# Routed expert rows: stores into four row slots per token, or additions into two tables of sums

## The reference

```
x = layernorm(x + attention(x))          # 16 heads of 16 channels, 4 key/value heads, causal
scores = sigmoid(x @ gate_w.T) + gate_b  # 16 experts
weights, indices = top_k(scores, 4); weights /= weights.sum()
shared = (silu(x @ w1_s) * (x @ w3_s)) @ w2_s
expert_e(x) = silu((x @ w1_e) * (x @ w3_e)) @ w2_e          # hidden width 176
x = layernorm(x + shared + sum over the 4 chosen e of weight_e * expert_e(x))
```

## Time and profile before

| | |
|---|---|
| runs of the kernel | 704.01 us median of 3 (700.44 to 706.06) |
| the profiled execution, its own time | 701.06 us |
| its span, first to last instruction | 699.3 us |
| mean granted PE clock | 0.894 of full speed |
| attention and routing | up to about 461 us of the span |
| expert stage | about 461 to 652 us |
| tail | about 652 to 699 us |

### The profile page before, as it was taken

The page is one execution under the profiler, slowest core; times in us unless marked ns, Lnnn a source line. Parts: engine busy times, 40 slices in busy tenths (PEclk is TensorE's granted clock), DMA queues, the critical chain, the costliest instruction groups (busy, mean ns, idle before and its releaser), DMA issues. The chain is left out here.

```text
span 699.3 us, 11914 instructions
## 1 busy us (share of the span) xinstructions
PE 561.5 (80%) x3708; PEld 363.4 (52%) x3708; DVE 454.6 (65%) x944; ACT 348.6 (50%) x759; POOL 307.3 (44%) x461
## 2 busy tenths in 40 slices
PE   4769987998899989589869877468999999999200
PEld 3434452443333544234323236458999999999100
DVE  4265537886775788578558116448777777776594
ACT  1216643566466557545555852235565666665022
POOL 3103324032743254836053731711677776776242
PEclk9959988899999999779798998869999999999655
DMA  4684614000511318212021232631344444441671
GB/s 117 114 186 68 98 42 63 6 25 1 132 40 40 47 43 156 73 40 94 1 74 58 65 88 62 203 97 47 98 136 126 126 128 120 130 131 36 240 300 60
DMA packets 53611, 64.92 MB, mean 93 GB/s; under 512 B 7995, under 2 KB 47310, under 8 KB 53552
## 3 DMA queue, kind: packets, MB, share of 16 engines
q1 hardware_dynamic: 46032, 46.45, 26.6%
q0 software_dynamic: 7104, 17.60, 7.1%
q10 hardware_dynamic: 416, 0.13, 0.1%
HBM read 32.49 MB, written 25.76 MB: 83 GB/s over the span
## 5 line engine op out<-in xcount | busy, mean ns | idle before, releaser
L1008 ACT ACTIVATE prob<-psT 128x512 f32<-128x512 f32 (+3 forms) x384 | 163.4, 496 | 107.3 <-PE psT L1521 101.8
L1230 DVE TENSOR_REDUCE MX<-psS 128x1 f32<-128x640 f32 (+6 forms) x176 | 175.7, 1027 | 47.5 <-PE psS L1556 45.3
L1552 PE MATMUL psS<-KS,QS 96*128 96x512 bf16 (+3 forms) x384 | 107.9, 362 | 18.9 <-DVE MX L1230 15.7
L1521 PE MATMUL psT<-QS,KS 98*128 98x512 bf16 (+3 forms) x384 | 106.5, 347 | 13.1 <-ACT prob L1008 8.2
L921 POOL TENSOR_SCALAR_AFFINE_SELECT prob<-prob 128x512 f32<-128x512 f32 x64 | 41.1, 643 | 139.9 <-ACT prob L1008 139.0
L973 POOL DMA_INDIRECT y_scratch<-ys,dst x80 | 80.9, 1011 | 37.8 <-POOL dst L966 18.7
L1536 PE MATMUL psO<-prob,V 128*32 128x512 f32 (+3 forms) x768 | 85.8, 521 | 8.9 <-POOL prob L921 7.2
L1726 PE MATMUL psH<-wU,xh 128*128 (+1 forms) x384 | 85.1, 345 | 9.3 <-issue 8.9
L892 POOL DMA_INDIRECT xs_scratch<-x1row,slotu x64 | 65.1, 1018 | 29.4 <-DVE slotu L1322 15.2
L1552 PEld LDWEIGHTS psS<-KS,QS 96*128 96x128 bf16 x384 | 34.1, 105 | 81.6 <-DVE MX L1230 46.8
L1726 PEld LDWEIGHTS psH<-wU,xh 128*128 128x128 f32 x384 | 65.3, 198 | 10.1 <-issue 10.1
(11 more groups left out here) (206 smaller groups left out, 983.3 us busy)
## 6 DMA issues: line engine op xcount, KB each, us to landing
xs<-xs_scratch SPq DMA_DIRECT2D x80, 134.0 KB
y<-y_scratch SPq DMA_DIRECT2D x8, 1024.0 KB, 12.3
QS<-qp SPq DMA_DIRECT2D x48, 128.0 KB, 4.6
wU_raw<-in_L_ffn_w_routed_dram SPq DMA_DIRECT2D x32, 176.0 KB, 3.4
xs_scratch<-padrow SPq DMA_DIRECT2D x1, 2144.0 KB
xs_scratch<-padrow SPq DMA_DIRECT2D x16, 134.0 KB
x1row<-in_L_attn_x_dram SPq DMA_DIRECT2D x4, 512.0 KB, 6.4
out_dram<-x1row SPq DMA_DIRECT2D x8, 256.0 KB, 2.1
```

The costliest lines, as they stand in the source:

```text
L1008: nc.scalar.activation(prob[:, step % NPROB, h, 0:HALF - c0], ps[:, 0:HALF - c0], ACT.Exp).then_inc(s_Tfree, 1)
L1230: nc.vector.tensor_reduce(out=MX[:, heads[0]:heads[-1] + 1, i - TH * q], in_=src, op=ALU.max, axis=AX_X).then_inc(s_Sfree, 1)
L1521: mm(ps[:, 0:HALF - c0], KS[b][:, g, j * P:(j + 1) * P], QS[:, QAT[(k // 2) % NSLOT], g % 2 * G + h, c0:HALF], start=True, stop=True).then ...
L1552: mm(ps[:, e * dist + c:e * dist + c + w], QS[0:ROWS, QAT[(k // 2) % NSLOT], g % 2 * G + h, (i - TH * q) * P:(i - TH * q + 1) * P], KS[b][ ...
```

## The change

`y4_scratch` (8192 rows) goes; two tables `y_sums0` and `y_sums1` of 2048 rows, one row per token, take its place. A tile's row is added in memory to the row of its token: tiles t = 0 go to table 0 and tiles t = 1 to table 1. As two additions to one row may not be under way together, each store of a table first waits until the store before it in the same table has landed. Both tables are set to zero first, by two DMAs of 2,048 KB each on SP's queue; the padding write of 2,144 KB moves together with them from behind qload 1 to behind qload 4. The tail loads two rows per token in 16 loads of 256 KB and does two additions where it did three. ACT and DVE wait, before they fill `ys` of pair n, for the store n - 2 of their own table alone.

```diff
-FAR = B * T * TOPK
+FAR = B * T
-    y4_dram = nc.dram_tensor("y4_scratch", (FAR, C), F32, kind="Internal").ap()
+    ya_dram = [nc.dram_tensor(f"y_sums{t}", (FAR, C), F32, kind="Internal").ap() for t in range(2)]
-        y4 = sb("y4", [P, NT, TOPK, C])
+        y2 = sb("y2", [P, NT, 2, C])
...
-                    if s == 1:
+                    if s == 4:
                         sp.wait_ge(s_const, CONSTS)
                         sp.dma_start(xs_dram[NE * REG:NE * REG + NE * P, :].rearrange("(m p) c -> p m c", p=P),
                                      padrow[:, :].unsqueeze(1).to_broadcast([P, NE, ROW])).then_inc(s_pad, 16)
+                        for t in range(2):
+                            sp.dma_start(ya_dram[t].rearrange("(i p) c -> p i c", p=P),
+                                         padrow[:, 0:C].unsqueeze(1).to_broadcast([P, NT, C])).then_inc(s_zero, 16)
...
             sp.wait_ge(s_up, EARLY + NRP)
-            for i in range(NYS):
-                sp.wait_ge(s_ysc[i], 32 * ((NRP - i + NYS - 1) // NYS))
-            y4_rows = y4_dram.rearrange("(i p k) c -> p i (k c)", p=P, k=TOPK)
+            for t in range(2):
+                sp.wait_ge(s_sum[t], 16 * NRP)
             for n in range(NSHP):
-                sp.dma_start(y4[:, 2 * n:2 * n + 2, :, :].rearrange("p i k c -> p i (k c)"),
-                             y4_rows[:, 2 * n:2 * n + 2, :]).then_inc(s_y4[n], 16)
+                for t in range(2):
+                    sp.dma_start(y2[:, 2 * n:2 * n + 2, t, :],
+                                 ya_dram[t][2 * n * P:2 * (n + 1) * P, :].rearrange("(i p) c -> p i c", p=P)).then_inc(s_y2[n], 16)
...
-            nc.gpsimd.iota(x1row[:, :, DT], pattern=[[P * TOPK, NT], [1, TOPK]], base=-FAR, channel_multiplier=TOPK,
+            nc.gpsimd.iota(x1row[:, :, DT], pattern=[[P, NT], [0, TOPK]], base=-FAR, channel_multiplier=1,
...
                     pool.wait_ge(s, EARLY + n + 1)
+                    if n:
+                        pool.wait_ge(s_sum[t], 16 * n)
+                    else:
+                        pool.wait_ge(s_zero, 32)
                     nc.gpsimd.indirect_dma_start(
-                        y4_dram, bass.IndirectOffsetOnAxis(ap=dst[:, n % NSEL, t:t + 1], axis=0),
-                        ys[:, n % NYS, t, :], None, bounds_check=FAR - 1, oob_is_err=False).then_inc(s_ysc[n % NYS], 16)
+                        ya_dram[t], bass.IndirectOffsetOnAxis(ap=dst[:, n % NSEL, t:t + 1], axis=0),
+                        ys[:, n % NYS, t, :], None, bounds_check=FAR - 1, oob_is_err=False,
+                        compute_op=ALU.add).then_inc(s_sum[t], 16)
...
-                    act.wait_ge(s_ysc[n % NYS], 32 * (n // NYS))
+                    act.wait_ge(s_sum[0], 16 * (n - NYS + 1))
...
-                    dve.wait_ge(s_ysc[n % NYS], 32 * (n // NYS))
+                    dve.wait_ge(s_sum[1], 16 * (n - NYS + 1))
...
-                dve.wait_ge(s_y4[n], 16)
-                link(nc.vector.tensor_tensor(y4[:, i, 0:2, :], y4[:, i, 0:2, :], y4[:, i, 2:4, :], ALU.add))
-                link(nc.vector.tensor_tensor(y4[:, i, 0, :], y4[:, i, 0, :], y4[:, i, 1, :], ALU.add))
-                link(nc.vector.tensor_tensor(x1[:, i, :], x1[:, i, :], y4[:, i, 0, :], ALU.add))
+                dve.wait_ge(s_y2[n], 32)
+                link(nc.vector.tensor_tensor(y2[:, i, 0, :], y2[:, i, 0, :], y2[:, i, 1, :], ALU.add))
+                link(nc.vector.tensor_tensor(x1[:, i, :], x1[:, i, :], y2[:, i, 0, :], ALU.add))
```

More of the change, by code:

```diff
@@ L639, in attention_moe @@
         s_sel = sem("s_sel")
-        s_ysc = [sem(f"s_ysc{i}") for i in range(NYS)]
-        s_y4 = [sem(f"s_y4_{i}") for i in range(NSHP)]
+        s_zero = sem("s_zero")
+        s_sum = [sem(f"s_sum{t}") for t in range(2)]
+        s_y2 = [sem(f"s_y2_{i}") for i in range(NSHP)]
         s_shift = sem("s_shift")
```

## The result

747.22 us, the median of 4 runs (745.35 to 748.89), against 704.37 us before: 1.0677 times before, 95% interval 1.0616 to 1.0737. The kernel got slower by 43 us; I had forecast 707.9 us with a range up to 745. The profiled execution has a span of 745.3 us against 699.3 us.

A forecast was written before the change was run, and what follows sets the result against it. PE was taken to set the 4.0 us expert-stage pair, with POOL having no reserve. Terms -11.1 - 2.75 + 17.7 + 0 = +3.85 us on the 704.01 us median gave 707.9 us, range 698 to 745.

The forecast's parts named there:

- Part 4 (b): Expert stage: POOL's own time per adding store stays unchanged at 0.99 to 1.05 us; upper end +0.5 us each.
- rival (B): Expert stage: POOL's store instruction gets longer; 724 us at 0.25 us per store, 742 at half as much again; chance 0.22.
- 2 us of buffer: Expert stage: two buffers of results absorb about 2 us of added POOL time, taken off the rivals' totals.
- Part 4 (a): Expert stage: an adding store lands 3.4 us after its start, costing nothing up to about 3.9 us; 0 us added.
- Part 3: Attention, SP's queue: padding and zeros behind qload 4 delay mrow 4 and stall PE; +17.7 us, ends 0 and +22.
- The 1 us for the clock: After the pause before head group 4: longer time at half clock speed, estimated at +1.0 us.
- Part 2: Attention start: without padding behind qload 1, PE no longer waits for mrow 0; -2.75 us, ends 0 and -4.
- Part 1: Tail: one large addition fewer per group and a shorter first load; -11.1 us, ends -8 and -13.
- Rival (C): SP's queue: no stall behind qload 4, as mrow 4 gets past or writes are much faster; 690 us, chance 0.08.
- (D): Tail: loads of 1 KB rows slower than DVE's 2.67 us lose 3 us of gain; 711 us, 0.07 with the rest.

The follow-up runs named there:

- experiment 4: Kernel before with two more small instructions per pair on POOL; 716.7 us, 22.9 us over its before, pairs 4.57 us.
- experiment 10: experiment 7 (plain, unordered stores) with POOL's choosing moved to DVE; 694.1 us (before 697.2), pairs 4.01 us.
- experiment 1: Changed kernel with plain overwriting stores, waits, tables and zero writes kept; 703.5 us (before 700.5), pairs 4.15 us.
- experiment 9: experiment 8 with three buffers of results instead of two; 1.0279 of before, pairs 4.89 us.
- experiment 5: Kernel before with padding moved behind qload 4 and two zero writes into unread tables behind it; 1.0167 of before, 11.6 us.
- experiment 2: Kernel before, stores adding without order into zeroed rows of their own, padding and zeros in 16 slices; 738.4 us, pairs 5.15 us.
- experiment 8: experiment 6 with the four small choosing instructions moved from POOL to DVE; 707.5 us, 1.0216 of before, pairs 4.85 us.
- experiment 11: experiment 2 with choosing on DVE and three buffers of results; 695.8 us (before 697.2), pairs 3.99 us.
- experiment 7: Kernel before with only its padding write moved, in 16 slices behind the mrow DMAs; 695.7 us, 0.9937 of before.
- experiment 3: experiment 6 with three buffers of results instead of two; 719.9 us, 1.038 of before, pairs 5.16 us.
- experiment 6: Changed kernel with padding and zeros in 16 slices, one behind each mrow DMA; 727.5 us, 1.0427 of before.
- experiment 12: experiment 9 with the tiles dealt to three tables in turn; 686.1 us, 0.9846 of before, pairs 3.99 us.

## Why the prediction was wrong

**What bounds the kernel.** Right. POOL had no reserve: 0.57 us more work on it made the pair 0.58 us longer (experiment 4). And PE set the pair beside it: with POOL's choosing taken away the pair stayed at 4.01 us (experiment 10).

**Part 4 (b) is the step that failed:** "I take it as unchanged, by the nearest row, which is the same instruction with the same 128 rows." The store that adds holds POOL for 1.57 to 1.59 us against 0.97 to 1.05, some +0.57 us, a little over my upper end of +0.5. Two of them and the missing reserve give 4.00 + 1.14 = 5.14 us per pair; the trace has 5.14 in an undisturbed pair and 5.23 in the mean. That is rival (B) at its upper price, to which I had given 742 us, and which had 0.22. That 742 lies near 747 is in part luck: the expert stage became 49 us longer and not 34, as the step was larger, all 39 steps counted and not 36, and no 2 us of buffer came off; the shorter pause and the shorter end of the program took 7 of these 15 us back.

The Trainium skill's rule, that a reduction in the DMA engines takes two read descriptors per piece ("Collectives: The Full Stack", The bandwidth ceiling), pointed the right way. The traces don't count descriptors; the time on POOL is 1.57 / 0.99 = 1.6 times the plain one and not twice. But they count packets. The line of the queue that POOL's stores use, from the page of experiment 1 (plain) and of the changed kernel (adding), with packets, MB and share of the DMA engines' time:

```profile
q0 software_dynamic: 7104, 17.60, 7.0%
q0 software_dynamic: 14784, 17.61, 13.7%
```

The addition makes 7,680 packets more of the same bytes, 96 for each of the 80 stores, and the queue's share of time about doubles. That these packets are what holds POOL for longer is likely, but no run shows it. I had the row that says POOL has no slack and an argument for a longer instruction, and weighed neither against a row that only shared the instruction's name.

**Part 4 (a)** was too small, 3.4 us taken and mostly 3.8 to 4.5 measured, and its point of decision was wrong as well. I had said that a landing costs nothing up to 3.9 us, as if the next store started at the landing. It starts 0.81 us later at the soonest (experiment 9), so the decision lies at about 4.00 - 0.81 = 3.2 us, and every usual landing of an adding store is over it. Plain stores, which the profiles of experiments 4 and 5 have at a median of 2.5 us, are under it, but single ones landed after as much as 4.1 us, and so the order still cost 0.16 us per pair (experiment 1). In the changed kernel this hardly shows, since (B) lies above it: without the order the pair is 5.15 (experiment 2), with it 5.13 to 5.23. It is the next bound at 4.85 to 4.89 us (experiments 8 and 9). The order itself can't simply go: "DMA: Bandwidth & Descriptors", Rules for kernel authors, in the Trainium skill, says that an accumulating DMA reads its destination and writes it later, and that another DMA's write which lands in between is lost. No run here shows that; experiments 2 and 11 give each row one addition.

**Part 3** was right in place and mechanism, +17.7 taken and 14.3 measured. The zeros moved at 386 GB/s where I had 335, which is 1.6 us of the difference. The 1 us for the clock doesn't show: with +11.9 in all, 14.3 - 2.75 leaves 0.3 us for it, less than two profiles differ by. **Part 2** was right: the 2.75 us are gone. Together +11.9 against +15.0, and +11.6 in experiment 5.

**Part 1** was right to the tenth, -11.1 us, though partly by luck: the last store landed 0.6 us later (2.71 us where it took 2.11), and the first group was there 3.7 us after its first issue where I had 4.3.

**Rival (C)**, a queue that lets mrow 4 past, fell with the 14.3 us. **(D)** fell as well, with DVE's step at 2.66 us.

## What to carry to other kernels

Before work is put on an engine, add up its own loop from the timeline, gaps included: POOL was 44% busy over the span and yet repeated at 4.00 us in a 4.00 us pair. The longest wait in the list need not be the cause: a buffer more took about 110 us of waiting away and nothing from the pair. Where transfers must be in order, what counts against the period is the landing and the time from there to the next start, 3.9 + 0.81 us here, and the long landings beside the usual one: three chains in turn hid what two could not. And a long write belongs in slices if anything small and urgent uses the same queue.

## What was unexpected in the hardware

- An indexed store of 128 rows of 1 KB holds POOL for 0.99 us (median; 0.97 to 1.05 in the kernel before), and for 1.54 to 1.58 if it adds (medians; single ones up to 1.81). From start to landing it is 2.5 us plain and 3.8 to 3.9 adding (medians); single landings took up to 4.1 and 5.5. The last stores, nearly empty, took 2.11 and 2.71 us.
- From a landing to the start of the next store that waited for it there are at least 0.81 us.
- SP's issues of the large zero writes took 10.33 us for two, and the next issue 5.31 us.
- The end of the program was 3.6 to 3.7 us shorter in every kernel with adding stores. The wait of SP's queue for PE's at the end of the program, in the kernel before:

```profile
SPq L419 <- PEq L419: 5.7, 1, 5.7
```

and in the changed kernel:

```profile
SPq L419 <- PEq L419: 2.0, 1, 2.0
```

  It is 5.7 again in experiment 1, which differs from the changed kernel by the addition alone, and in experiments 4, 5, 7 and 10, which add nothing; it is 2.0 or 2.1 in experiments 2, 3, 6, 8, 9, 11 and 12. Why stays open.
